# A transformer decoder layer on one core: another table for when the weights are split during the first sequence

## The reference

```python
x = x + _L0_attn_ref(_layernorm(x, axis=-1), L0_attn_Wq, L0_attn_Wk, L0_attn_Wv, L0_attn_Wo)
x = x + _L0_xattn_ref(_layernorm(x, axis=-1), ctx_1024, mask_BxS_ik0, L0_xattn_Wq, L0_xattn_Wkv, L0_xattn_Wout, L0_xattn_bout)
x = x + _L0_ffn_ref(_layernorm(x, axis=-1), L0_ffn_Wg, L0_ffn_We, L0_ffn_be)
# inside each attention, per head:
attn = jax.nn.softmax(jnp.einsum('bhqd,bhkd->bhqk', q, k) * scale, axis=-1)
out = jnp.einsum('bhqk,bhkd->bhqd', attn, v)
```

## Time and profile before

| | |
|---|---|
| median of 3 runs | 3596.63 us |
| the profiled execution's own time | 3596.79 us |
| its span | 3595.0 us, at a mean granted clock of 0.993 |
| busy share of the span: PE, DVE, ACT, POOL | 97%, 66%, 62%, 59% |
| chain that ended last: PE, DVE, issue | 89%, 6%, 2% |

### The profile page before, as it was taken

The page is one execution under the profiler, slowest core; times in us unless marked ns, Lnnn a source line. Parts: engine busy times, 40 slices in busy tenths (PEclk is TensorE's granted clock), DMA queues, the critical chain, the costliest instruction groups (busy, mean ns, idle before and its releaser), DMA issues.

```text
span 3595.0 us, 80997 instructions
## 1 busy us (share of the span) xinstructions
PE 3499.9 (97%) x28992; PEld 2955.3 (82%) x28992; DVE 2361.6 (66%) x7401; ACT 2220.9 (62%) x6442; POOL 2121.0 (59%) x1928
## 2 busy tenths in 40 slices
PE   6899999999999999999999999999999999999997
PEld 5788888888888888888888888888888888888886
DVE  6666667666676666676666666666766666666664
ACT  5666666666666666666665766656666657666563
POOL 5555666555675556665556765566655567655661
PEclk8999999999999999999999999999999999999999
DMA  3100000000000000000000000000000000000000
GB/s 98 37 10 13 10 9 10 10 12 12 7 11 11 9 12 12 6 10 10 12 12 7 13 10 9 12 13 6 10 10 12 12 6 13 10 9 12 13 6 8
DMA packets 46796, 47.44 MB, mean 13 GB/s; under 512 B 8256, under 2 KB 43328, under 8 KB 46400
## 3 DMA queue, kind: packets, MB, share of 16 engines
q1 hardware_dynamic: 45696, 41.99, 4.0%
q10 hardware_dynamic: 704, 0.27, 0.0%
HBM read 33.86 MB, written 8.39 MB: 12 GB/s over the span
## 4 chain that ended last, share of the span: by engine, by line
PE 89%; DVE 6%; issue 2%; POOL 2%; ACT 2%; DMA 0%; ACTq 0%; POOLq 0%; DVEq 0%
PE unit_ps L536 19%; PE pT_ps L648 14%; PE oT_ps L665 14%; PE score_ps L632 11%; PE wo_ps L690 10%; PE unit_ps L546 9%; PE unit_ps L524 9%; DVE x L1021 2%; ACT probs L798 1%; POOL probs L1150 1%; DVE probs L936 1%; PE unit_ps L555 1%; DVE bn L863 1%; DVE x_in L1029 1%; DVE w_lo L851 0%
## 5 line engine op out<-in xcount | busy, mean ns | idle before, releaser
L1150 POOL TENSOR_TENSOR probs<-probs,inv_sum 128x512 f32<-128x512 f32 x1024 | 1062.0, 1041 | 967.3 <-DVE inv_sum L919 967.2
L787 ACT ACTIVATE pT<-pT_ps 128x512 f32<-128x512 f32 x1024 | 605.9, 594 | 135.9 <-PE pT_ps L648 135.4
L798 ACT ACTIVATE probs<-probs,neg_max 128x256 f32<-128x256 f32 x1024 | 508.7, 499 | 277.5 <-DVE probs L936 277.5
L648 PE MATMUL pT_ps<-ident,probs 128*128 128x128 f32 x4096 | 635.3, 280 | 13.0 <-POOL probs L1150 12.4
L648 PEld LDWEIGHTS pT_ps<-ident,probs 128*128 128x128 f32 x4096 | 452.9, 141 | 221.6 <-issue 204.1
L798 ACT ACTIVATE probs<-score_ps,neg_max 128x256 f32<-128x256 f32 x1024 | 476.5, 476 | 179.1 <-DVE neg_max L925 179.1
L665 PE MATMUL oT_ps<-pT,v_sb 128*64 128x256 f32 x4096 | 555.9, 392 | 3.8 <-ACT pT L787 3.5
L936 DVE TENSOR_SCALAR_CACHE_REDUCE probs<-score_ps,mask_add 128x256 f32<-128x256 f32 x1024 | 433.5, 480 | 105.8 <-PE score_ps L632 102.8
L536 PE MATMUL unit_ps<-xs_hi,w_lo 128*128 128x256 f32 x1536 | 460.2, 300 | 8.7 <-DVE swap L972 7.2
L536 PE MATMUL unit_ps<-xs_hi,w_hi 128*128 128x256 f32 x1536 | 436.9, 284 | 0.0
L536 PE MATMUL unit_ps<-xs_lo,w_hi 128*128 128x256 f32 x1536 | 436.3, 284 | 0.0
(11 more groups left out here) (121 smaller groups left out, 8422.2 us busy)
## 6 DMA issues: line engine op xcount, KB each, us to landing
x_in<-dram_x SPq DMA_DIRECT2D x32, 256.0 KB, 2.7
xn<-dram_ctx SPq DMA_DIRECT2D x32, 256.0 KB, 2.7
layer_out<-x SPq DMA_DIRECT2D x32, 256.0 KB, 2.2
swap<-dram_bout SPq DMA_DIRECT2D x32, 128.0 KB, 3.3
rope<-dram_be SPq DMA_DIRECT2D x32, 64.0 KB, 3.1
rope<-dram_we SPq DMA_DIRECT2D x5, 256.0 KB, 2.9
probs<-dram_sk SPq DMA_DIRECT2D x4, 256.0 KB, 4.4
x<-dram_cq SPq DMA_DIRECT2D x4, 256.0 KB, 2.8
```

The costliest lines, as they stand in the source:

```text
L648: last = nc.tensor.transpose(pT_ps[s % 2][:, k * T + t * P:k * T + (t + 1) * P], probs[:, hs % P_BUFS, t, k * P:(k + 1) * P], ident[:])
L787: nc.scalar.activation(flat(pT[:, s % 2, :, :]), pT_ps[s % 2][:], ACT.Copy).then_inc(pT_ready.sem, 1)
L798: last = nc.scalar.activation(dst, src, ACT.Exp, bias=neg_max[:, h % STATS, t:t + 1], scale=1.0 if h < H else -1.0, accum_out=row_sum[:, h ...
L1150: nc.gpsimd.tensor_tensor(weights, weights, inv.unsqueeze(2).to_broadcast([P, NT, T]), ALU.mult).then_inc(probs_ready.sem, 1)
```

## The change

Only the two tables are changed. `FIRST` now has 27 pieces and `LATER` 13; before it was 20 and 20. The order of the pieces and their contents are the same.

```diff
-FIRST = {24: 2, 26: 1, 27: 1, 28: 1, 29: 2, 30: 1, 32: 1, 33: 5, 35: 6}
-LATER = [(1, 0), (2, 0), (4, 0), (6, 0), (9, 0), (10, 1), (11, 0), (13, 0), (14, 1), (15, 0), (16, 1), (17, 0),
-         (17, 1), (18, 0), (19, 0), (20, 1), (21, 0), (22, 1), (24, 1), (29, 1)]
+FIRST = {24: 1, 26: 3, 27: 1, 28: 1, 29: 2, 30: 3, 32: 7, 34: 7, 35: 2}
+LATER = [(2, 0), (4, 0), (6, 0), (8, 0), (10, 0), (12, 0), (14, 0), (16, 1), (17, 0), (18, 0), (18, 1),
+         (19, 0), (26, 1)]
```

## The result

The changed kernel takes 3589.10 us, the median of 15 runs (3587.29 to 3590.16), against 3595.16 us for 15 runs of the kernel before (3591.95 to 3597.58). The ratio is 0.9983 with a 95% interval of 0.9975 to 0.9990: 6.1 us, or 0.17%, faster. The sign was forecast, the size was not (-2.5 us), and the time lies 0.7 us under the range.

The account below looks back on a forecast made before the run. It took DVE to bound the prologue from about 16 us on, and PE the later sequences, unchanged. Prologue cost +2.7 and sequence 0 gain 5.2 made -2.5 us, so 3594.1 us, range 3589.8 to 3599.

Parts of the forecast that it names:

- Gain: sequence 0: Sequence 0, which seven splits leave: shorter PE waits for exponentials or heads, gain 5.2 us, bounds 1.5 and 7.9.
- Rival 1: Sequence 0: all 7.9 us of PE waits go and the clock stays up, 3.3 us more; 3588.1 us, chance 0.15.
- slots 20 and 21: Sequence 0: high and low part delay the reciprocal, PE waits 1.93 us for that head; gain taken as 1.1 us.
- about two thirds: Sequence 0: share of PE's waits counted as gain, since without expert work some would show again behind another cause.
- slot 15: Sequence 0: a split in an odd slot behind PE's wait of 0.85 us; gain taken as 0.5 us.
- The prologue: Stretch up to the first exponential: DVE-bound, seven pieces added ahead of the row maxima, cost +2.7 us.
- Step 1: Prologue up to Q0: the norm goes sooner, so Q0's first matmul starts 1.0 us sooner, bounds 0 to 1.8.
- step 2: Prologue, DVE from Q0 to the row maxima: 27.35 us against 23.6, with 10.5 us of excess beside POOL.
- the full exclusion: Prologue, shared port: each DVE and POOL meeting costs a whole POOL operation, 1.3 us not 1.0; cost +3.4.
- The parity argument: Sequence 0: odd-slot splits precede the next pair's row maxima and lead to scores; even-slot splits only delay a reciprocal.
- Rival 2: Sequence 0: POOL's chain holds the pace, gain only 1.5 against cost 3.4; slower at 3598.5 us, chance 0.25.
- Rival 3: Prologue: loads bind, each of three ring turns 1.5 us longer, cost 7.2; slower at 3598.6 us, chance 0.1.

Follow-up runs that it names:

- first experiment: Kernel before plus 30 extra matmuls on idle PE ahead of the slot 2 scores of sequence 0, splits unchanged: 3593.54 us against 3595.75, not resolved.
- second experiment: Kernel before with only `FIRST` changed: its 20 early pieces in the new table's slots, old `LATER` kept: 3590.67 us against 3595.75.
- sixth experiment: Changed kernel plus 16 extra matmuls on PE at slot 18 of sequence 0, while it waits for the norm: 3589.04 us against 3589.10.
- eighth experiment: Kernel with all 40 pieces in the prologue, plus 70 extra matmuls on PE ahead of the slot 2 scores: 3598.95 us, as without the matmuls.
- the third: Changed kernel with seven later pieces moved one slot ahead, from slots 2, 4 to 14 to slots 1, 3 to 13: 3593.71 us.

## Why the prediction was wrong

**The failed step is the one under "Gain: sequence 0" that counted only PE's waits**, put PE's clock at nothing and left it to rival 1. Between slots 14 and 24 it gave 1.6 us, and 5.6 came: 3.6 of them are the clock, 2.0 the splits.

*How the two are told apart.* I cut slots 14 to 24 once more, at rows of PE that all profiles have: the first scores of slot 14 (81.18 in the first profile of the kernel before), the first product with the values that waited behind it (88.74), the first matmul of the last output projection of self-attention (95.75), the transposes behind the norm (101.26), the scores of slot 20 (107.56), the first turned head of cross-attention (113.22) and the scores of slot 24 (118.61). Times in us, means over three profiles for before and after; the other columns are single profiles:

| from | before | first experiment | second experiment | after, second profile | after, mean | difference of the means |
|---|---|---|---|---|---|---|
| slot 14 | 7.56 (low) | 6.00 | 6.00 | 6.01 | 6.21 | -1.35, clock |
| product with the values | 7.02 | 7.02 | 7.03 | 6.10 | 6.11 | -0.91, splits |
| output projection | 5.50 | 5.51 | 5.50 | 5.52 | 5.51 | 0 |
| transposes | 6.34 (low) | 6.45 (low) | 6.45 (low) | 5.25 | 5.67 | -0.67, clock |
| slot 20 | 5.66 | 5.66 | 5.65 | 4.53 | 4.53 | -1.13, splits |
| turned head | 5.40 (low) | 5.39 (low) | 4.36 | 3.86 | 3.86 | -1.54, clock |

The first row is the clock's: the first and second experiments have the old splits, no low stretch there, and the length of the changed kernel. So is the fourth: the sixth experiment has 5.25 at full clock. In the last one PE has no wait at all in either kernel, and runs the same matmuls (first profile before, then after):

```profile
113.22:118.61 5.39, 5.39 (x32) 5.25 (x32) 4.80 (x16) 4.03 (x12) 2.09 (x3) 0.68 0.30 86
108.43:112.28 3.85, 3.85 (x32) 3.72 (x32) 3.45 (x13) 3.21 (x11) 1.89 (x2) 1.00 0.03 11
```

With the old splits and the full clock it is 4.36 (second experiment): there the clock alone gives 1.0, and the other 0.5 us come only when the splits are gone too. The windows of the first row (before, first experiment, second profile after), then of the fourth (first profile after, sixth experiment):

```profile
81.18:88.74 7.56, 7.18 (x41) 5.62 (x41) 3.45 (x7) 4.91 (x15) 1.61 (x2) 0.60 0.12 35
80.27:86.27 6.00, 4.83 (x41) 3.57 (x41) 3.31 (x7) 4.93 (x15) 1.62 (x2) 1.00 0.15 44
80.48:86.49 6.01, 4.72 (x40) 3.62 (x41) 3.06 (x7) 4.36 (x13) 2.53 (x3) 1.00 0.34 87
```

```profile
97.41:103.90 6.49, 5.03 (x29) 4.86 (x29) 3.23 (x6) 2.31 (x4) 0.00 (x0) 0.74 0.27 81
100.06:105.31 5.25, 3.73 (x28) 3.37 (x29) 3.22 (x6) 2.32 (x4) 0.00 (x0) 1.00 0.32 100
```

*The splits' share* is 0.9 us at slots 14 to 20, where I had 0.5, and 1.1 at slots 20 and 21, where I had 1.1. So the discount to "about two thirds" was wrong for slot 15, where PE's wait of 0.85 went whole, and the delay at slots 20 and 21 was priced right. Of the missing 4.0 us, 3.6 are the clock and 0.4 this.

*Rival 1* had a clock price of 3.3 us, near the 3.6 that were found, but by luck: it took all of it from the window 66.7 to 92, where the low stretch of 6.8 us was worth 1.6 (7.56 to 6.00), and had nothing for the stretches at 101 and 114. It was also wrong in having all waits go: PE still waits 0.8 us at four places. Its mechanism was part of the truth, and should have stood in the likeliest case.

*Do the low stretches follow from the waits?* Over all profiles they go together. From slot 13 to 23 the six with waits of 1.6 and 1.3 us ahead of slot 14 have 13.7 us at the low clock (three times), 6.8, 3.4 and 3.4. The eight without these waits have 6.8, 3.4, 3.4 and five times none. But in no experiment were the waits changed and all else kept, so this is not shown.

*What held.* The prologue: +2.37 against +2.7. Step 1 gave 1.5 us (Q0's first matmul at 10.24 and not 11.77) where I had 1.0: the wait for the third piece's load, for which I took back 0.8, did not come. In step 2 the excess beside POOL was 9.7 us by the groups of the profile after against 10.5; DVE needed 27.1 us from behind Q0 to the row maxima, forecast 27.35. By the full exclusion that the Trainium skill states ("SBUF — State Buffer", section "Who interferes with whom") the cost would have been +3.4; the trace has 1.0 us a meeting and not 1.3. The parity argument gave slots 10 to 14 within 0.1 us and was confirmed by moving splits by one slot. From slot 24 to the last output projection nothing changed.

*Rival 2* (POOL holds sequence 0) is right for slots 2 to 10 alone, where only 0.2 us came. In slots 2 to 4 the low clock with no split at slot 1 takes 6.96 to 7.56 us, the full clock with a split there 6.70, and the full clock without it 5.29. That looks like two chains of about the same length side by side, of which removing one gives little. It is not shown: the 5.29 stands in one profile, the eighth experiment failed to make it again, and the third has 6.32 with a split at slot 1 and 3.4 us at the low clock. Even the 1.7 us of that one profile came back in part, since its slots 4 to 10 took 18.23 us and not 17.40. *Rival 3* did not come: ACT waited for loads up to 1.4 us in the prologue, but DVE waited behind it only at the first piece (0.47 us).

*What stays open* is why the clock fell at slot 13 in the kernel before and not in two kernels with the same splits and the same waits of 1.6 and 1.3 us ahead of it.

## What to carry to other kernels

Where work is moved out of a stretch, first ask which places in that stretch it stood in front of something. Here moving all later splits to harmless slots took 7.4 us off and cost nothing in the prologue, where the change took 6.1 (the intervals overlap, but its scores of sequence 1 come 1.3 to 1.9 us sooner); with a better prologue it was 9.0. Where the profile shows a low granted clock beside waits of PE, the low stretch is a term of its own in the sum: price it window by window, and give it a chance to go with the waits. Before a difference of a few microseconds in one profile is explained, take a second profile of the same kernel, and look whether its runs were all granted the same clock.

## What the runs showed of the hardware

- A subtraction of two SBUF operands of 128 x 512 on DVE takes 0.61 us from start to start when alone, and about 1.0 us more for each GpSimd operation that it meets (17 pieces with 7.9 us of excess over 8 operations before, 23 with 9.7 over 10 after); the GpSimd sum takes 1.6 us in place of 1.26.
- The same instructions ran at 2.4 GHz from the first scores of slot 2 on in one execution, and at 1.2 GHz for the first 4.3 to 6.3 us in others (slots 2 to 4 of the changed kernel: 5.29, then 6.96 and 7.13, and 7.56 us in the sixth experiment). The Trainium skill ("TensorE: Matmul & The Clock Gate", section "Part 1: The HAM clock gate (the "warmup" mystery)") says that activity releases the throttle. The trace agrees: with 30 matmuls that ended 1.45 us before the scores of slot 2 these ran at the full clock. 70 that ended 3.74 us before them raised the clock too, but it was low again when the scores began.
- 5.39 us in which PE never waited took 3.85 at the full clock, with 3.4 us of the 5.39 at 1.2 GHz. Where PE does wait, a low stretch costs less: one of 6.8 us was worth 1.6.
